# Six joined layers on one core: the norm's factors by one power, and a quantised layer with products that nothing reads

## The reference, cut to what matters

```python
x = _layernorm(x + _L0_attn_ref(x, ...))     # "hy" and "up" in the kernel: down, two scans, up
x = _layernorm(x + _L0_xattn_ref(x, ...))    # "ca": cross attention
x = _layernorm(x + _L0_ffn_ref(x, ...))      # "ff": quantised layer
x = _layernorm(x + _L1_attn_ref(x, ...))     # "sa": self attention
x = _layernorm(x + _L1_xattn_ref(ctx, x, ...))  # "de", "st", "yy": recurrent decoder
x = _layernorm(x + _L1_ffn_ref(x, ...))      # "rf": routed layer with signs as weights
```

```python
def _dynamic_quant(x, inv_smooth):
    xs = x.astype(jnp.float32) * inv_smooth
    scale = jnp.maximum(jnp.max(jnp.abs(xs), axis=-1, keepdims=True) / QMAX, 1e-08)
    q = jnp.clip(jnp.round(xs / scale), -QMAX, QMAX)
    return (q, scale)
x_flat = x.reshape(-1, H).astype(jnp.bfloat16)                 # 2048 rows of 1024
qg, sg = _dynamic_quant(x_flat, inv_gate)
qu, su = _dynamic_quant(x_flat, inv_up)
gate_out = (qg @ w_gate.T) * sg * s_wgate[None, :]             # 512 columns
up_out = (qu @ w_up.T) * su * s_wup[None, :]
inter = jnp.clip(jax.nn.silu(gate_out) * up_out, -10.0, 10.0).astype(jnp.bfloat16)
qi, si = _dynamic_quant(inter, inv_inter)
out = (qi @ w_down.T) * si * s_wdown[None, :]                  # 1024 columns
```

## Time and profile before

| | |
|---|---|
| median of 3 runs | 3969.88 us (3968.72 to 3972.8) |
| profiled execution, its own time | 3982.61 us |
| its span, first to last instruction | 3980.8 us |
| TensorE busy in the span | 80% |
| VectorE, ScalarE, GpSimd busy | 56%, 40%, 13% |
| granted TensorE clock, mean | 0.90 of full |

### The profile page before, as it was taken

How to read it: one execution, slowest core, us unless ns; L and a number is a source line. 1 busy time by engine, 2 the same in 40 slices (tenths; PEclk the granted TensorE clock), 3 DMA queues, 4 the chain that set the end, 5 groups by cost and what they waited for, 6 DMA issues and landing times. The chain is left out here.

```text
span 3980.8 us, 109362 instructions
## 1 busy us (share of the span) xinstructions
PE 3182.8 (80%) x43218; PEld 2136.2 (54%) x43218; DVE 2233.0 (56%) x5375; ACT 1579.2 (40%) x3982; POOL 502.0 (13%) x1854
## 2 busy tenths in 40 slices
PE   7556568644479999999688899999999999985797
PEld 4424135322256666666344666666666666662343
DVE  2656767578855555555421555555555555547455
ACT  2221134444522222222111566666666666652333
POOL 0000321133310000000000000000000000005232
PEclk9576679866789999999899999999999999996799
DMA  2000020110010000000101233333333333320100
GB/s 97 3 1 1 11 45 8 39 52 0 0 45 1 0 0 0 0 0 0 35 29 37 78 91 87 91 90 88 91 87 92 86 92 88 90 84 0 66 32 37
DMA packets 278942, 176.69 MB, mean 44 GB/s; under 512 B 14496, under 2 KB 268016, under 8 KB 278816
## 3 DMA queue, kind: packets, MB, share of 16 engines
q1 hardware_dynamic: 276128, 172.70, 14.8%
q0 software_dynamic: 2752, 3.18, 0.5%
HBM read 165.12 MB, written 13.90 MB: 45 GB/s over the span
## 5 line engine op out<-in xcount | busy, mean ns | idle before, releaser
L1828 PE MATMUL ps<-de_hg,st_at 128*32 128x128 f32 x16384 | 516.3, 275 | 0.3 <-DVE st_at L1990 0.3
L1828 PEld LDWEIGHTS ps<-de_hg,st_at 128*32 128x32 f32 x16384 | 424.5, 110 | 31.6 <-DVE st_at L1990 0.5
L1893 ACT ACTIVATE st_th<-ps,st_sw 128x128 f32<-128x128 f32 x1024 | 292.7, 368 | 248.0 <-PE ps L1800 248.0
L1973 DVE TENSOR_TENSOR st_th<-ps,st_sw 128x512 f32<-128x512 f32 x256 | 177.1, 692 | 155.5 <-PE ps L1800 155.5
L1766 POOL COPY de_ah<-st_at 128x8 f32 (+1 forms) x256 | 50.7, 198 | 1510.2 <-DVE st_at L1990 1510.2
L1247 PEld LDWEIGHTS ps<-sa_xt,w_wq 128*128 128x128 f32 x2048 | 234.7, 194 | 11.0 <-issue 9.2
L1247 PE MATMUL ps<-sa_xt,w_wq 128*128 128x128 f32 x2048 | 237.9, 278 | 1.9 <-ACT sa_xt L1363 1.9
L1318 PE MATMUL ps<-sa_wo,sa_ct 128*128 128x512 f32 x512 | 225.0, 598 | 13.1 <-issue 13.1
L1789 PE MATMUL ps<-st_hk,st_cwt 112*32 112x128 f32 x4096 | 164.7, 278 | 87.9 <-DMA st_hk<-padded_alignments 85.9
L2252 PE MATMUL ps<-rf_wb,rf_sp 128*128 128x512 bf16 x768 | 184.4, 394 | 20.1 <-DVEq L2383 20.1
L1800 PE MATMUL ps<-st_fs,st_waf 32*128 32x128 f32 x4096 | 186.5, 296 | 12.5
(11 more groups left out here) (415 smaller groups left out, 6341.3 us busy)
## 6 DMA issues: line engine op xcount, KB each, us to landing
st_hk<-padded_alignments SPq DMA_DIRECT2D x254, 448.0 KB, 3.6
X<-in_x_dram SPq DMA_DIRECT2D x16, 512.0 KB, 9.0
out_dram<-X SPq DMA_DIRECT2D x16, 512.0 KB, 2.7
w_wq<-in_Wq_perm_dram SPq DMA_DIRECT2D x1, 4096.0 KB
sa_wo<-in_Wo_perm_dram SPq DMA_DIRECT2D x1, 4096.0 KB, 14.2
gate_inputs<-dp_ro SPq DMA_DIRECT2D x16, 256.0 KB, 2.3
st_rin<-gate_inputs SPq DMA_DIRECT2D x128, 32.0 KB, 3.3
rf_wf<-in_weightT_dram SPq DMA_DIRECT2D x8, 512.0 KB, 8.0
```

What stands on the lines that cost most here:

```text
L1828: ins = pe.matmul(R[g][32 * q:32 * q + 32, :], at[g][:, b, :], hg[:, BG * g + b, q * P:(q + 1) * P], start=False, stop=(b == BG - 1), tile ...
L1893: ins = act.activation(th[g][:, b, :], sums(g, 0)[:, b // 2, (b % 2) * P:(b % 2 + 1) * P], ACT.Tanh, bias=sw[g][:, b:b + 1])
L1973: dve.tensor_tensor(th[g][:, 4:8, :].rearrange("p (k s) n -> p k s n", s=2), sums(g, 1).rearrange("p k (s n) -> p k s n", s=2), sw[g][:, 4 ...
```

## The change

It has two parts.

**The norm, in all six stages.** VectorE stops after `bn_aggr`. GpSimd makes minus the mean, adds epsilon, raises the sum to the power -0.5 in one instruction (`ALU.pow`), and multiplies: four instructions in place of thirteen, and none of VectorE's five.

```diff
     def statistics(self, dve, link, k):
...
-        link(dve.bn_aggr(self.agg[:, k, :], self.stats[:, k, :, :]))
-        v, y, nm = self.vy[:, k, 0:1], self.vy[:, k, 1:2], self.vy[:, k, 3:4]
-        link(dve.tensor_scalar(v, self.agg[:, k, 1:2], LN_EPS, None, ALU.add))
-
-        link(dve.tensor_scalar(y.bitcast(I32), v.bitcast(I32), 1, None, ALU.logical_shift_right))
-        link(dve.tensor_scalar(y.bitcast(I32), y.bitcast(I32), -1.0, float(0x5F3759DF), ALU.mult, ALU.add))
-        link(dve.tensor_scalar(v, v, -0.5, None, ALU.mult))
-        dve.tensor_scalar(nm, self.agg[:, k, 0:1], -1.0, None, ALU.mult).then_inc(self.var_done, 1)
+        dve.bn_aggr(self.agg[:, k, :], self.stats[:, k, :, :]).then_inc(self.agg_done, 1)
 
     def factors(self, pool, link, b, k):
 
-        pool.wait_ge(self.var_done, b + 1)
-        v, y, q, nm = (self.vy[:, k, n:n + 1] for n in range(4))
-        for step in range(3):
-            link(pool.tensor_tensor(q, y, y, ALU.mult))
-            link(pool.tensor_tensor(q, q, v, ALU.mult))
-            link(pool.tensor_tensor(q, q, self.c15[:, :], ALU.add))
-            link(pool.tensor_tensor(self.rs[:, k, 0:1] if step == 2 else y, y, q, ALU.mult))
+        pool.wait_ge(self.agg_done, b + 1)
+        eps, power, minus = (self.consts[:, n:n + 1] for n in range(3))
+        v, nm = self.vy[:, k, 0:1], self.vy[:, k, 1:2]
+        pool.tensor_tensor(nm, self.agg[:, k, 0:1], minus, ALU.mult)
+        link(pool.tensor_tensor(v, self.agg[:, k, 1:2], eps, ALU.add))
+        link(pool.tensor_tensor(self.rs[:, k, 0:1], v, power, ALU.pow))
         pool.tensor_tensor(self.rs[:, k, 1:2], nm, self.rs[:, k, 0:1], ALU.mult).then_inc(self.rstd_done, 1)
```

```diff
+            def turn_half(pe, b, n):
+                j, h = divmod(n, 2)
+                if h == 0:
+                    pe.wait_ge(added, 2 * b + j + 1)
+                if n == 0 and has(b - 1):
+                    pe.wait_ge(t_kept, 3 * b)
+                elif n == 2 and has(b - 1):
+                    pe.wait_ge(t_kept, 3 * b - 1)
+                elif n == 3:
+                    pe.wait_ge(t_kept, 3 * b + 1)
+                for k in range(4):
+                    ins = pe.transpose(ps[:, (0, 1, 2, 0)[n], k * P:(k + 1) * P],
+                                       v[:, j, (4 * h + k) * P:(4 * h + k + 1) * P], ident[:, :])
+                ins.then_inc(t_done, 1)
+            def keep_warm(pe, bank, n):
+                for _ in range(n):
+                    pe.matmul(ps[:, bank, :], identb[:, :], wd[:, 0, 0:512], start=True, stop=True)
+
+            def project(pe, b, j):
+                if j == 0:
+                    pe.wait_ge(gu_used, b)
+                    keep_warm(pe, GU, 4)
+                else:
+                    keep_warm(pe, GU + 1, 3)
+                pe.wait_ge(t_kept, 3 * b + (1, 3)[j])
+                for k in range(KH):
+                    ins = pe.matmul(ps[:, GU + j, :], qt[:, j, k, :], (wu if j else wg)[:, k, :],
+                                    start=(k == 0), stop=(k == KH - 1))
+                ins.then_inc(gu_done, 1)
...
                 def body(b, k):
-                    if has(b + 1):
-                        gate_and_up(pe, b + 1)
-                    pe.wait_ge(qi_done, b + 1)
+                    pe.wait_ge(added_i, b + 1)
+                    pe.wait_ge(qit_done, b)
                     for m in range(KF):
...
                     ins.then_inc(ti_done, 1)
+                    pe.wait_ge(dn_used, b)
+                    keep_warm(pe, DN, 3)
                     pe.wait_ge(qit_done, b + 1)
...
                     ins.then_inc(dn_done, 1)
+                    if has(b + 1):
+                        for n in range(3):
+                            turn_half(pe, b + 1, n)
+                        project(pe, b + 1, 0)
+                        turn_half(pe, b + 1, 3)
+                        project(pe, b + 1, 1)
+                        pe.wait_ge(dn_used, b + 1)
+                        keep_warm(pe, DN, 12)
```

```diff
-                for dst, src in ((swg, "s_wgate"), (swu, "s_wup"), (swd, "s_wdown"), (invi, "inv_inter")):
+                for n, src in enumerate(("inv_gate", "inv_up")):
+                    sp.dma_start(inv[:, n, :], a[src].partition_broadcast(P)).then_inc(i_load, 16)
+                for dst, src in ((swg, "s_wgate"), (swu, "s_wup"), (invi, "inv_inter"), (swd, "s_wdown")):
                     sp.dma_start(dst[:, :], a[src].partition_broadcast(P)).then_inc(w_load, 16)
```

More of the change, by code:

```diff
@@ L928, in _ @@
             def _(pool):
-                pool.wait_ge(w_load, 96)
-                def smooth(b, k):
-                    pool.wait_ge(staged, b + 1)
-                    if not (isinstance(b, int) and b < 2):
-                        pool.wait_ge(q_done, 2 * b - 2)
-                    for j in range(2):
-                        pool.tensor_tensor(v[:, k, j, :], xh[:, k, :], inv[:, j, :], ALU.mult).then_inc(scaled, 1)
                 ln.start_pool(pool, Chain(pool, pool_seq))
-                for b in range(4):
-                    smooth(b, b % 2)
@@ L941, in _ @@
-                with pool.Fori(0, NB // 2 - 2) as i:
-                    link = Chain(pool, pool_seq, 1 + i * 2 * ln.POOL_LINKS)
+                with pool.Fori(0, NB // 2) as i:
+                    link = Chain(pool, pool_seq, ln.POOL_SETUP + i * 2 * ln.POOL_LINKS)
                     for k in range(2):
                         ln.factors(pool, link, 2 * i + k, k)
-                        smooth(2 * i + 4 + k, k)
-                link = Chain(pool, pool_seq, 1 + (NB - 4) * ln.POOL_LINKS)
-                for b in range(NB - 4, NB):
-                    ln.factors(pool, link, b, b % 2)
@@ L989, in stage16, with add_round, off, keep_gate @@
                 if not (isinstance(b, int) and b < 2):
[L990 removed]
+                    act.wait_ge(read, b - 1)
                 act.copy(xh[:, k, :], tile_of(b)).then_inc(staged, 1)
[L993 removed]
+            def add_round(act, b, j):
                 act.wait_ge(rc_done, 2 * b + j + 1)
[L995 to L1005 removed]
+                act.activation(v[:, j, :], v[:, j, :], ACT.Identity, bias=rnd[:, 0:1], scale=rc[:, j:j + 1]).then_inc(added, 1)
+            def off(act, dst, src):
+                return act.activation(dst, src, ACT.Identity, bias=rnd[:, 1:2])
+            def keep_gate(act, b):
+                act.wait_ge(t_done, 4 * b + 2)
+                act.wait_ge(gu_done, 2 * b)
+                off(act, qt[:, 0, :, :].rearrange("p k n -> p (k n)"), ps[:, 0:2, :].rearrange("p a n -> p (a n)")).then_inc(t_kept, 1)
+            def keep_up(act, b):
+                for h in range(2):
+                    act.wait_ge(t_done, 4 * b + 3 + h)
+                    off(act, qt[:, 1, 4 * h:4 * h + 4, :].rearrange("p k n -> p (k n)"), ps[:, (2, 0)[h], :]).then_inc(t_kept, 1)
             @block.scalar
@@ new lines, in _, with body @@
+                dve.wait_ge(w_load, 64)
+                FIRST = 6
+                PER = 4 + 2 + 6 + 2 + ln.LINKS
+                state = {"link": link}
+                def body(b, k):
+                    link = state["link"]
+                    dve.wait_ge(gu_done, 2 * b + 1)
+                    dve.scalar_tensor_tensor(out=gu[:, 0, :], in0=ps[:, GU, :], scalar=sc[:, 0:1], in1=swg[:, :],
+                                             op0=ALU.mult, op1=ALU.mult).then_inc(gate_done, 1)
+                    dve.wait_ge(gu_done, 2 * b + 2)
+                    link(dve.scalar_tensor_tensor(out=gu[:, 1, :], in0=ps[:, GU + 1, :], scalar=sc[:, 1:2], in1=swu[:, :],
+                                                  op0=ALU.mult, op1=ALU.mult))
+                    dve.sem_inc(gu_used, 1)
+                    dve.wait_ge(silu_done, b + 1)
+                    link(dve.tensor_tensor(gu[:, 1, :], gu[:, 0, :], gu[:, 1, :], ALU.mult))
+                    link(dve.tensor_scalar(it[:, :], gu[:, 1, :], LIMIT, -LIMIT, ALU.min, ALU.max))
+                    dve.wait_ge(ti_done, b)
+                    link(dve.tensor_tensor(vi[:, :], it[:, :], invi[:, :], ALU.mult))
+                    find_scale(dve, link, vi[:, :], 2 + k, rci_done)
+                    if has(b + 1):
+                        for j in range(2):
+                            smooth(dve, link, b + 1, 1 - k, j)
@@ L1121, in start @@
+                    ln.statistics(dve, link, k)
+                    if not isinstance(b, int) and k == 1:
+                        assert link.n == 2 * PER, (link.n, PER)
                 def start(i):
-                    state["link"] = Chain(dve, dve_seq, FIRST + (2 * i + 1) * PER)
+                    state["link"] = Chain(dve, dve_seq, FIRST + (2 * i + 2) * PER)
                 over_tiles(dve, body, start)
-                form_row(state["link"], LAST, 1)
-                ln.statistics(dve, state["link"], 1)
```

174 lines of the change are left out of this document (53 added, 121 removed).

## The result

The changed kernel takes 3834.12 us (median of 4 runs, 3831.79 to 3836.29), the kernel before 3969.3 us (4 runs, 3965.87 to 3972.8): ratio 0.9659, 95% interval 0.9643 to 0.9676.

A forecast was written before the change was run, and what follows sets the result against it. TensorE bounds sa and rf, VectorE up and yy; in ff VectorE is busiest, TensorE's clock 0.69. Norm tiles 50.6, stage ends 16, quantised layer 34.6: 101.2 us, so 3969.9-101 = 3869 us; 8-in-10 range 3838 to 3915.

The forecast's parts named there:

- Up, yy: Tiles of up and yy: without five short instructions they run at VectorE's 4.44 us pitch, gaining 17.6 and 18.7 us.
- Ca: 14.3 for the tiles: Tiles of ca: 0.95 us less before the copy that TensorE waits for, 15x0.95 = 14.3 us.
- I give nothing for it, since TensorE covers it: Norm in the tiles of sa and rf: no gain, TensorE being busy 97% and 91%.
- The ends: Ends of up, ca, sa, yy and rf: `bn_aggr` to apply 1.3 us instead of 4.5, 5x3.2 = 16 us.
- Ff, entry 9.8: Start of the quantised layer: smoothing rows load first, gate's first products end at 801.2 instead of starting at 811.0; 9.8 us.
- Ff, tiles 20.1: Tiles of the quantised layer: pitch 18.8 us instead of 20.14, gain 15x(20.14-18.8) = 20.1 us.
- rival 2: Quantised layer: the clock never falls, 17.7 us a tile, kernel at 3852 us; chance 0.14 (with ca's clock).
- the 1.1 us for "every second tile" at 2.2: Ff tiles: a clock fall after TensorE's second gap costs 2.2 us every second tile, raising 17.7 to 18.8.
- the two holes: TensorE's idle gaps in an ff tile: 1.9 us before the inner rows, 1.5 us before up's rounding ends.
- Rival 1: Ff: dummies don't hold the clock, pitch 25.4 us, kernel 3968 us (half the tiles: 3918); chance 0.17 in any measure.
- Rival 4: Ff: the products are of no use since VectorE binds anyway; no gain in the body, 3887 us; chance 0.03.
- Rival 3: GpSimd's power is dear, up's and yy's pitch (6.7+X)/2, all gain gone at X = 5.5; chance 0.04, beyond 5 us 0.02.

The follow-up runs named there:

- Experiment 6: Changed kernel with five short chained instructions put back on VectorE after `bn_aggr` in all six norms, results unused: 3894.23 us, ratio 0.9787 to the kernel before.
- Experiment 7: Changed kernel with nine more chained one-column instructions on GpSimd ahead of the power, results unused: 3893.62 us, ratio 0.9784 to the kernel before.
- experiment 8: Changed kernel with each tile's two smoothing products given back to GpSimd, VectorE waiting for them: 3864.38 us, ratio 0.9715 to the kernel before.
- experiment 12: Changed kernel with twenty dummy products in place of the twelve behind up's product and none of the ten others: 3830.99 us, ratio 0.9642 to the kernel before.
- experiments 1 and 11: 1: changed kernel without any of its 22 dummy products, 3840.27 us; 11: without the twelve behind up's product, the ten others kept, 3839.78 us.

## Why the prediction came out as it did

The direction and the larger part of each mechanism held; the size was short by a third, and the steps that failed are terms of the sum.

- **Up, yy.** 17.6 for up's tiles; measured (84.2-67.7) = 16.5, and the whole stage 20.5 of 20.8. For yy 16.0 instead of 18.7: its tiles alternate between 4.47 and 4.75, and the shorter one is the 4.44 that was counted. GpSimd and ScalarE's apply are covered, as said. What makes the second one longer wasn't tried.
- **Ca: 14.3 for the tiles was too little.** 217.1-198.0 = 19.1 was measured: 13.20 instead of 13.52 a tile. The 0.95 was right (13.93 to 12.93 in a quiet tile), and what was left "in the range", the falls of the clock in TensorE's idle time, belonged in the sum. (They come behind the 1.9 us of idle that every second tile has; the earlier trace rows shows the 1.68 of the others.) Before there were three tiles of 15.79 among tiles of 14.4, after none: 4.1 us. Experiment 6 puts the five instructions back and both the pitch and the 0.97 return. The 13.20 is a little flattering: its first tile took 13.43 us, in eight other executions with the new norm 15.0, which makes the pitch 13.31. Some 2.8 of the stage's 25.0 lie ahead of the first tile and weren't looked into.
- **Rf: "I give nothing for it, since TensorE covers it" is the step that was wrong outright.** 12.9 us came from the tiles (15.48 to 14.88 in a quiet one, 9 in all, and 4 from the four that had been slow) and some 3 from the end. TensorE's 91% said that nine tenths are its own; the other tenth, 20 us in 15 waits for VectorE, was the kernel's to win, and the norm's chain on GpSimd led there by way of ScalarE's queue. Experiment 7 shows the owner.
- **Sa.** 5.1 instead of 3.2. The stage took 840.8 to 842.4 us in the three executions with the old norm and 835.5 to 839.3 in the ten with the new one and without the nine extra steps, so 3.2 may well be right.
- **The ends.** 3.2 each; 3.13 at ca (4.48 to 1.35). The power at 0.55 for 0.3 was made good by the hand-overs.
- **Ff, entry 9.8:** 10.6. VectorE starts at 744.12, 5.5 us after the stage does; gate's first products take 2.94 instead of 3.6, since the clock rises within them.
- **Ff, tiles 20.1: mis-sized, 34.7 measured.** The chain itself was right to 0.2 us (17.5 in quiet tiles for 17.7), so rival 2's pitch of 17.7 was nearly what came. The term that failed is the 1.1 us for "every second tile" at 2.2: three tiles in fifteen were longer, by 1.7, which makes 0.34. The mechanism is there in those three (a second hole of 1.78 us, then gate's products slowed). But the prediction counted the two holes apart, and they aren't: where the clock falls at the first, the slower down products fill the second, and 0.5 to 0.7 us of it are left.
- **Ff, exit 4.7:** 3.7. The down products took 2.71 us, not 1.90: the twelve dummies ended 2.23 us too soon.
- **Rival 1** (the products don't hold the clock, 3968) assumed that they are needed and lie on the path. Without any of them the time is the same. **Rival 4** (of no use) had the right fact with the wrong reason and price: VectorE is busy 206 of 267 us and isn't the bound; the path alternates between VectorE, ScalarE and TensorE, and its TensorE parts, gate's and up's products, have the full clock anyway. **Rival 3** needed 5.5 us for a power. Its formula for up's pitch was short, as experiment 7 shows: it gives (6.7+0.55+2.43)/2 = 4.84 us with nine more instructions, and 5.24 was measured.

What the layer gained, then, came from taking the smoothing off GpSimd (experiment 8: 16 of its 49 us) and the entry (10.6); the rest, some 22 us, is left to the end of the norm (about 3), the three clips, the separate `q` and `qi` and the order of the two bodies, which weren't taken apart. The products, the part that gives the change its name, bring nothing that the time shows as they stand, and by the pitches ten of them cost what twelve bring.

## What to carry to other kernels

An engine that is busy 91% of a stage doesn't cover the other engines' chains: ask what the remaining waits end on, and follow that chain through the queue of every engine it passes. Work that only keeps TensorE busy shortened the layer here where it filled a hole (twelve products, 0.65 us a tile), and took as much back where it stood in front of products on the path; so try it place by place and compare with none. A clock that rises in the profile is not a gain by itself.

## What the runs showed of the hardware

The blocking of VectorE by GpSimd goes both ways. In experiment 8 GpSimd's product held up VectorE's. In the kernel before, at the end of ff, a GpSimd step over one column that else takes 0.19 us took 1.05, while VectorE added two rows in SBUF:

```profile
1127.76 1.23 DVE L1089 TENSOR_TENSOR ff_row<-ff_row,X 128x1024 f32<-128x1024 f32 x1 [0.16 <-DVE ff_row L1086]
1127.98 1.05 POOL L113 TENSOR_TENSOR ff_vy<-ff_vy 128x1 f32<-128x1 f32 x1
```

A power on GpSimd over one column costs 0.55 us, its neighbours there 0.19. And whether the clock falls behind a hole of TensorE isn't told by the hole's length alone. In ff a hole of 2.24 to 2.39 us was followed by half clock in most tiles of the changed kernel and by full clock in three. A hole of 1.78 us was followed by half clock in those three; in experiment 12 every tile but the first has one of 1.78 us, and the clock stays full. In rf before, 1.4 to 1.6 us were followed by a fall in four tiles and not in the others; in ca, 1.9 us in three. The holes of 4.8 to 5.0 us of experiments 1 and 11 were followed by half clock each time, those of 0.8 us in rf after never.
